# Output projection's first terms inside the context attention, and its norm, the quantised linear and the next norm as one stage worked by halves

## The reference

```python
x = x + xattn0(layernorm(x), ctx)      # causal attention, then attention to the context, 16 heads of 16; output projection Wp, bp
x = x + linear0(layernorm(x))          # FP6 (E2M3) block-quantised linear: 256 -> 256
x = x + attn1(layernorm(x))            # hyperbolic attention; starts with W_qkv

def _mx_quantize(t, eps=1e-30):        # blocks of 32 elements share a scale
    scales = jnp.maximum(jnp.max(jnp.abs(blocks), axis=-1) / FP6_E2M3_MAX, eps)
    q = _nearest_on_grid(blocks / scales[..., None], _GRID)
out = xd @ wd.T + bias                 # xd, wd: quantised and scaled back
```

## Time and profile before

| | us |
|---|---|
| median of three runs (4047.57 to 4056.62) | 4048.33 |
| the profiled execution's own time | 4053.46 |
| its span, first to last instruction | 4051.7 |
| from the divide's last instruction (L1335) to De's first product (L2122), batch 1 | 46.74 |
| TensorE matmul busy over the span | 3359.0 (83%) |
| VectorE busy over the span | 2079.9 (51%) |
| ScalarE busy over the span | 1633.4 (40%) |
| GpSimd busy over the span | 919.6 (23%) |

### The profile page before, as it was taken

The page is one execution under the profiler, slowest core; times in us unless marked ns, Lnnn a source line. Parts: engine busy times, 40 slices in busy tenths (PEclk is TensorE's granted clock), DMA queues, the critical chain, the costliest instruction groups (busy, mean ns, idle before and its releaser), DMA issues. The chain is left out here.

```text
span 4051.7 us, 56156 instructions
## 1 busy us (share of the span) xinstructions
PE 3359.0 (83%) x21550; PEld 1837.2 (45%) x21550; DVE 2079.9 (51%) x4231; ACT 1633.4 (40%) x2349; POOL 919.6 (23%) x961
## 2 busy tenths in 40 slices
PE   6887788988887788988887888988876888947997
PEld 4325545254334535254234543263254452436886
DVE  5655665634655665634746555535656556430111
ACT  3353833333445642433437542433538333411221
POOL 1202822011105522012116420012018220140111
PEclk9998799999997898999997998999997999958998
DMA  4102012011202022011220121012120121134554
GB/s 116 55 13 78 1 45 89 20 38 45 59 24 55 1 49 84 20 43 40 59 69 11 32 71 51 19 24 60 38 78 1 45 72 37 35 126 159 172 180 150
DMA packets 227190, 239.73 MB, mean 59 GB/s; under 512 B 95542, under 2 KB 193956, under 8 KB 224612
## 3 DMA queue, kind: packets, MB, share of 16 engines
q1 hardware_dynamic: 219552, 215.73, 18.3%
q10 hardware_dynamic: 3620, 10.07, 0.7%
q0 software_dynamic: 3744, 10.26, 0.7%
HBM read 167.24 MB, written 68.76 MB: 58 GB/s over the span
## 5 line engine op out<-in xcount | busy, mean ns | idle before, releaser
L867 ACT ACTIVATE prob<-psum 128x1024 f32<-128x1024 f32 x384 | 372.2, 1021 | 509.0 <-PE psum L785 509.0
L1235 ACT ACTIVATE prob<-psum 128x1024 f32<-128x1024 f32 (+3 forms) x384 | 331.6, 914 | 363.8 <-PE psum L1136 363.8
L913 DVE TENSOR_REDUCE scr<-psum 128x1 f32<-128x512 f32 x576 | 369.0, 685 | 195.9 <-PE psum L772 192.1
L1275 DVE TENSOR_REDUCE stats<-psum 128x1 f32<-128x512 f32 (+3 forms) x576 | 331.9, 619 | 140.9 <-PE psum L1124 137.7
L782 PE MATMUL psum<-stack 32*128 32x512 f32 x1536 | 226.5, 660 | 15.2 <-ACT prob L867 10.4
L398 PE MATMUL psum<-ident 128*128 128x128 f32 x1704 | 213.5, 280 | 0.0
L398 PEld LDWEIGHTS psum<-ident 128*128 128x128 f32 x1704 | 203.7, 195 | 14.9 <-issue 13.8
L1124 PE MATMUL psum<-stack 96*128 96x512 bf16 (+3 forms) x576 | 181.8, 364 | 31.5 <-DVE stats L1275 31.1
L815 PE MATMUL psum<-prob,ones_f 128*32 128x512 f32 x1536 | 202.1, 594 | 0.0
L1151 PE MATMUL psum<-prob,vbig 128*32 128x512 f32 (+3 forms) x1536 | 189.4, 566 | 4.2 <-ACT prob L1235 4.2
L2832 PE MATMUL psum<-xgT,ew 128*128 128x256 f32 x736 | 167.8, 387 | 18.0 <-DVE xgT L2880 18.0
(11 more groups left out here) (483 smaller groups left out, 6495.9 us busy)
## 6 DMA issues: line engine op xcount, KB each, us to landing
ew<-in_L_ffn_W SPq DMA_DIRECT2D x46, 1024.0 KB, 7.8
stack<-q_terms SPq DMA_DIRECT2D x144, 128.0 KB, 2.5
w_mlp<-in_L_xattn_a_li_w SPq DMA_DIRECT2D x16, 1024.0 KB, 6.2
q_terms<-parts SPq DMA_DIRECT2D x96, 128.0 KB, 2.2
stack<-k_terms SPq DMA_DIRECT2D x72, 128.0 KB, 2.9
stack<-k_terms SPq DMA_DIRECT2D x36, 256.0 KB, 4.4
w_mlp<-a_terms SPq DMA_DIRECT2D x36, 256.0 KB, 4.7
a_keys<-stack SPq DMA_DIRECT2D x4, 2048.0 KB, 6.3
```

What stands on the lines that cost most here:

```text
L867: act.activation(prob[:, i % 4, :, :], psum[:, 2 * p:2 * p + 2, :], ACT.Exp, scale=scale).then_inc(exped, 1)
L913: dve.tensor_reduce(found[:, c:c + 1], ring(i), AX.X, ALU.max).then_inc(freed, 1)
L1235: act.activation(prob[:, i % 4, :, q0:T], psum[:, 2 * p:2 * p + 2, q0:T], ACT.Exp, scale=scale).then_inc(exped, 1)
L1275: dve.tensor_reduce(found[:, c:c + 1], ring(i)[:, 0:keys_of(t)], AX.X, ALU.max).then_inc(freed, 1)
```

## The change

1. Of the 16 products of the output projection, the 12 for head groups 0 to 2 move into the last group of the context attention (`join_attention`): two ahead of each of the last four `weigh`, and four in place of `keep_running` beside the division. The bias row is added on GpSimd early in the same stage (`add_bias`).
2. `norm("Bo")`, "Cq" and `norm("Co")` become one stage "Cq". Two barriers go. The last four products of the output projection open it; the projections of keys and values follow at once.
3. The norms, the transposes, the copies and the products of the linear are done by halves of two tiles. VectorE joins two tiles with one instruction. The linear's bias is added on GpSimd beside the quantising.
4. `quantise` handles a list of parts, here two halves in turn, and `chained(..., behind=1)` waits for the instruction before the last, which belongs to the same half. Six instructions behind the rounding become four. The set-up's use of `quantise` on the weight gets the shorter form in one part.
5. Fillers on TensorE: 20, then 10, 4 and 6 of `keep_running`, in place of 11 and 5.

```diff
@@ -70,14 +70,15 @@
-def chained(eng, sem):
...
     def then(ins):
         count[0] += 1
         ins.then_inc(sem, 1)
-        eng.wait_ge(sem, count[0])
+        if count[0] > behind:
+            eng.wait_ge(sem, count[0] - behind)
     return then
@@ -224,36 +225,47 @@
...
-    def quantise(dve, then, src, n, a, b_, c_, amax, scale, rscale):
...
-        then(dve.tensor_scalar(src, a, MAGIC, None, ALU.add))
-        then(dve.tensor_scalar(src, src, MAGIC, None, ALU.subtract))
-
-        then(dve.tensor_tensor(b_, src, a, ALU.subtract))
-        then(dve.tensor_scalar(b_, b_, 0.5, None, ALU.is_ge))
-        then(dve.tensor_tensor(src, src, b_, ALU.subtract))
-        then(dve.tensor_tensor(src, src, c_, ALU.mult))
-        then(dve.tensor_tensor(s3, s3, scale.unsqueeze(2).to_broadcast(wide3), ALU.mult))
+    def quantise(dve, then, settled, parts, done):
...
+        for src, n, a, b_, c_, amax, scale, rscale in parts:
+            then(dve.tensor_reduce(amax, blocks(src), AX.X, ALU.max, apply_absolute_value=True))
...
+        for src, n, a, b_, c_, amax, scale, rscale in parts:
+            then(dve.tensor_scalar(src, a, MAGIC, None, ALU.add))
+        for src, n, a, b_, c_, amax, scale, rscale in parts:
+            then(dve.scalar_tensor_tensor(b_, src, MAGIC, a, ALU.subtract, ALU.subtract))
+        for src, n, a, b_, c_, amax, scale, rscale in parts:
+            then(dve.scalar_tensor_tensor(src, b_, 0.5, src, ALU.is_ge, ALU.subtract))
+        for src, n, a, b_, c_, amax, scale, rscale in parts:
+            then(dve.scalar_tensor_tensor(src, src, MAGIC, c_, ALU.add, ALU.mult))
+        settled()
+        for src, n, a, b_, c_, amax, scale, rscale in parts:
+            dve.tensor_tensor(blocks(src), blocks(src), per_block(scale, n), ALU.mult).then_inc(done, 1)
@@ -1182,14 +1195,25 @@
...
+                    if g == HG - 1 and kt >= 4:
+                        if kt == 4 and next_products:
+                            pe.wait_ge(divided, HG - 1)
+                        for t, k in next_products[2 * kt - 8:2 * kt - 6]:
+                            join_attention(pe, t, k)
                     weigh(n)
                     if kt == 2 and g:
                         spread_inverses(pe, g - 1, inverted, spread_in)
                     for ev in during[n][1]:
                         event(ev)
-                keep_running(pe, 3, 3)
+                for t, k in next_products[8:10]:
+                    join_attention(pe, t, k)
+                if not next_products:
+                    keep_running(pe, 3, 3)
                 gather(HG - 1)
-                keep_running(pe, 2, 3)
+                for t, k in next_products[10:]:
+                    join_attention(pe, t, k)
+                if not next_products:
+                    keep_running(pe, 2, 3)
                 spread_inverses(pe, HG - 1, inverted, spread_in)
                 keep_running(pe, 6, 3)
@@ -1245,6 +1269,8 @@
...
+                if beside is not None:
+                    beside(pool)
...
+    def join_attention(pe, t, k):
+        return pe.matmul(psum[:, 4 + t // 2, t % 2 * C:(t % 2 + 1) * C], yT[:, k, t * P:(t + 1) * P], wBp[:, k, :],
+                         start=(t % 2 == 0 and k == 0), stop=(k == HG - 1), skip_group_check=True)
@@ -2027,6 +2058,10 @@
...
+    def add_bias(pool):
+        for t in range(QT):
+            pool.tensor_tensor(x[:, t, :], x[:, t, :], e.R["L0_xattn_bp"], ALU.add)
...
+                   stack[:, 4096:12288].rearrange("p (s j n) -> p s j n", s=2, j=J), add=e.colB[:, 0, :], ready=ready,
+                   next_products=[(t, k) for t in range(QT) for k in range(HG - 1)], beside=add_bias)
...
+def fp6_linear(e):
...
+    with stage(nc, "Cq", "joined", "added", "var_ready", "rstd_ready", "dc", "normed", "biased", "quant", "turned", "xT_in", "summed",
+               "projected", "taken", "x_turned") as (
+            block, joined, added, var_ready, rstd_ready, dc, normed, biased, quant, turned, xT_in, summed,
+            projected, taken, x_turned):
         @block.sync
         def _(sp):
+            load_mlp(e, sp, 1)
             sp.wait_ge(taken, 2 * HG)
             sp.dma_start(e.a2_keys, e.work[:, 4096:8192]).then_inc(e.a2_stored, 16)
             sp.wait_ge(taken, len(jobs))
             sp.dma_start(e.a2_values, e.work[:, 0:4096]).then_inc(e.a2_stored, 16)
         @block.tensor
         def _(pe):
+            def turn(h, bank):
+                for k in range(KT):
+                    for t in HALVES[h]:
+                        c = k * N + t % 2 * P
+                        last = pe.transpose(psum[:, bank, c:c + P], xh[:, t, k * P:(k + 1) * P], ident[:, :])
+                return last
+            for h in range(2):
+                for t in HALVES[h]:
+                    last = e.join_attention(pe, t, HG - 1)
+                last.then_inc(joined, 1)
             pe.wait_ge(e.kv_loaded, 32)
             for i, (kind, g, h) in enumerate(jobs):
                 if i >= 4:
                     pe.wait_ge(taken, i - 3)
+                bank = psum[:, i % 4, :]
                 if kind == "k":
                     last = pe.matmul(bank, e.w2k[:, 0, g * P:(g + 1) * P], e.cnT[:, 0, h * BANK:(h + 1) * BANK],
                                      start=True, stop=True)
                 else:
                     last = pe.matmul(bank, e.cnT[:, 0, g * P:(g + 1) * P], e.w2v[:, 0, :], start=True, stop=True)
                 last.then_inc(projected, 1)
+            pe.wait_ge(taken, len(jobs))
+            e.keep_running(pe, 20, 0)
+            for h in range(2):
+                pe.wait_ge(quant, h + 1)
+                turn(h, 6 + h).then_inc(turned, 1)
+            for h in range(2):
+                pe.wait_ge(xT_in, h + 1)
+                pe.wait_ge(added, h + 1)
+                for t in HALVES[h]:
+                    for k in range(KT):
+                        last = pe.matmul(of_half(h)[:, t % 2, :], xT[:, k, t * P:(t + 1) * P], e.wC[:, k, :],
+                                         start=(t % 2 == 0 and k == 0), stop=(k == KT - 1), skip_group_check=True)
+                last.then_inc(summed, 1)
+            for h in range(2):
+                e.keep_running(pe, (10, 4)[h], 0)
+                pe.wait_ge(normed, 2 * QT - 2 + 2 * h)
+                turn(h, 6 + h).then_inc(x_turned, 1)
+            e.keep_running(pe, 6, 0)
         @block.scalar
         def _(act):
             for i, (kind, g, h) in enumerate(jobs):
                 act.wait_ge(projected, i + 1)
+                bank = psum[:, i % 4, :]
                 if kind == "v":
                     act.copy(values[:, g, :], bank).then_inc(taken, 1)
                     continue
                 act.copy(keys[:, g, h * BANK:(h + 1) * BANK], bank).then_inc(taken, 1)
+            for h in range(2):
+                act.wait_ge(turned, h + 1)
+                act.copy(xT[:, :, h * N:(h + 1) * N], psum[:, 6 + h, :].rearrange("p (k n) -> p k n", k=KT)).then_inc(xT_in, 1)
+            for h in range(2):
+                act.wait_ge(x_turned, h + 1)
+                act.copy(xT[:, :, h * N:(h + 1) * N], psum[:, 6 + h, :].rearrange("p (k n) -> p k n", k=KT))
+        @block.gpsimd
+        def _(pool):
+            def inverse_root(n, h):
+                pool.wait_ge(var_ready, n)
+                s = slice(2 * h, 2 * h + 2)
+                pool.tensor_tensor(rstd[:, s], eps_var[:, s], e.nhalf[:, 0:2], ALU.pow).then_inc(rstd_ready, 1)
+            inverse_root(1, 0)
+            inverse_root(2, 1)
+            for h in range(2):
+                pool.wait_ge(normed, 2 * h + 2)
+                for t in HALVES[h]:
+                    ins = pool.tensor_tensor(x[:, t, :], x[:, t, :], R["L0_ffn_bias"], ALU.add)
+                ins.then_inc(biased, 1)
+            inverse_root(3, 0)
+            inverse_root(4, 1)
+        @block.vector
+        def _(dve):
+            counted = [0]
+            then = chained(dve, dc, 0, counted)
+            then_other_half = chained(dve, dc, 1, counted)
+            def join(h):
+                dve.tensor_tensor(tiles(x, h), of_half(h), tiles(x, h), ALU.add).then_inc(added, 1)
+            def variance(h, n):
+                dve.wait_ge(added, n)
+                for t in HALVES[h]:
+                    last = dve.bn_stats(stats[:, t, :], x[:, t, :])
+                then(last)
+                for t in HALVES[h]:
+                    last = dve.bn_aggr(mv[:, t, :], stats[:, t, :])
+                then(last)
+                s = slice(2 * h, 2 * h + 2)
+                dve.tensor_scalar(eps_var[:, s], mv[:, s, 1], EPS, None, ALU.add).then_inc(var_ready, 1)
+            def normalise(h, n):
+                dve.wait_ge(rstd_ready, n)
+                for t in HALVES[h]:
+                    dve.tensor_scalar(xh[:, t, :], x[:, t, :], mv[:, t, 0:1], rstd[:, t:t + 1],
+                                      ALU.subtract, ALU.mult).then_inc(normed, 1)
+            for h in range(2):
```

(17 more changed lines are left out.)

95 lines of the change are left out of this document (48 added, 47 removed).

## The result

The changed kernel takes 3992.97 us, the median of four runs (3988.82 to 3995.69), beside 4052.47 us for the kernel before on the same chip (4047.57 to 4057.63). The ratio is 0.9853, with a 95% interval from 0.9839 to 0.9867. The profiled execution took 3994.16 us with a span of 3992.4.

What follows compares the result with a forecast made beforehand. Bound by a serial chain between barriers: last products and join, VectorE's norm and quantising, then a relay between engines. Four batches at 8.8 us plus 3 for the clock gave 38 off 4048.33: 4010 us, range 3998 to 4028.

Steps and rivals of the forecast that it cites:

- Rival B: TensorE's clock drops behind the quantising after 2.4 us idle: 5 us a batch, 4030 us if in all; chance 0.10.
- The clock in De: Next stage opens mostly at 2.4 GHz: 1.75 us saved in two batches, 3.5, of which 3 us booked.
- 4 x 8.8: Gain per batch in four batches: 3.8 us at the quantising's start, 2.0 in it, 3.0 behind it.
- A's spacing: Quantising halves do not overlap, instructions 0.73 and 0.46 us apart: 3.2 us more a batch, 4023 us; chance 0.11.
- C's steps of over 3.2 us: Early products in the context attention's last group do not hide: 2.6 us a batch, 4020 us; chance 0.03.
- E's queue: TensorE's in-order work in the stage, at 1.2 GHz throughout, ends 16.6 us a batch later: 4115 us; chance 0.04.
- D's loss: A later wait takes back the gain, so the change does nothing: 4036 to 4060 us; chance 0.06.
- GpSimd's work in a batch: Bias additions, 2.78 us on GpSimd, land where it was idle for 124.75 us: nothing booked.
- P: Follow-up theory: time outside the stage depends on where low-clock stretches fall against unchanged stages once a batch's length changes.

Runs made afterwards that it cites:

- a_pool14: Changed kernel with 14 tiny GpSimd instructions added in the context attention, where GpSimd is idle: 4004.4 us, ratio 0.9896.
- b_pool242: Kernel before with 242 tiny GpSimd instructions added in the context attention, where GpSimd is idle: 4039.13 us, ratio 0.9975.
- better: Changed kernel with early products one step earlier and by head group, linear's bias on GpSimd later, two fillers for four: 3977.74 us, ratio 0.9829.
- b_barrier: Kernel before with one semaphore cleared once more at the end of the second MLP unit: 4038.09 us, ratio 0.9974.
- wait_each: Changed kernel with each quantising instruction waiting for the one ahead, also across the halves: 4012.35 us, ratio 0.9917.
- after: The changed kernel itself, against the kernel before: 3992.97 us, ratio 0.9853.

## Why the prediction was off

**Right.** The stage opened 1.94 us after the divide. From there to the quantising 7.47 us passed (312.81 to 320.28), against 7.8. The instructions of the quantising are 0.61 and 0.34 us apart (322.08 to 323.30 for two, 324.50 to 325.17 for two), as taken from the one pair of neighbours that did not wait; half 0 was ready after 15.07 us (15.4 forecast), half 1 after 15.61 (16.0). The Trainium skill's VectorE: DVE Perf Modes, § Rules for kernel authors, would have instructions few rather than their waits. Here a wait one instruction back was worth 3.5 us a batch with the count unchanged, so on the waits the measurement speaks against it; on the count it agrees, for 32 short instructions with a wait on each took 19.1 us, where 18 long ones took 17.5. Behind the quantising the forecast had 12.2 us; batch 2 took 12.0, batch 1 13.5. Normalising beside the additions took 1.54 us, for a forecast 1.5. What the barriers that went are worth by themselves, no run shows; the sum over all the steps came out.

**Off in size, small.** The early products delay the last weighing by 0.99 us (300.94 to 305.13 is 4.19, against 3.20 in the earlier trace rows), not 0.6: between a score and a weighing two products take 1.06 us from start to start, not 0.86, and in the last step the pair started as the exponentials came. The context attention grew by 0.95 us a batch. Rival B came in part: the clock fell behind the quantising in two batches of four and cost 1.5 us each, where I had 5. The clock in De was sized at 3 us and the part up to Do gained 5.4; De's first four products take 1.95 or 1.96 us in all four batches. The stage and the context attention gained 36.9 - 3.8 = 33.1 us together, where 4 x 8.8 = 35.2 were forecast. That all this gives 38.5 for 38 is in part luck: one term was 2.1 too high and the other 2.4 too low. Of the other rivals, A's spacing, C's steps of over 3.2 us and E's queue did not show, and D's loss was a gain of the opposite sign.

**The step that failed** is the sum, "4 x 8.8 + 3 = 38 us": it books nothing for stages that the change doesn't touch, and the range goes down only by what could go better inside the stage. 20.8 us came from outside.

- 8 to 11 us: GpSimd's first instruction behind the loop's jump, late by 2.2 to 3.3 us a batch before and by 0.2 to 0.3 after, because its program is 14 instructions shorter. In the two profiled executions the three sections differ by 7.8 us together. `a_pool14`, which gives the lateness back, is 11.4 us slower than the changed kernel, and `b_pool242` 11.2 faster than the kernel before, of which its trace shows 5.9 in the sections. The prediction dealt with GpSimd's work in a batch ("nothing") and looked at no row of the next batch's first stage, where GpSimd's root starts 1.9 us after its variance is ready.
- The other 10 to 13 us stay open: 7.0 between the two MLP units, 1.9 in batch 1's first stage, 4.1 in the rest. Between the MLP units the same instructions took 223.2 to 223.7 us in 55 of the 80 batches of all 20 traces, and 224.9 to 227.0 in the other 25, `better`'s batch 2 (226.75) among them. The kernel before was long in three of its four batches, the changed kernel in none. But the kernel before and those made from it were long in 13 of 24 batches, with an average of 224.39 us, and the changed kernel and those made from it in 12 of 56, with 223.85. By these averages the change would win 2.2 us there, not 7.0; the rest is that these two executions fell far apart, as P has it. Why long batches are rarer with the change no run shows.

Open: which block of GpSimd's program is missing at the jump, and why 14 instructions decide it; the traces show one more load of instructions 0.2 to 0.9 us behind the branch at every jump of the six kernels that are late there (the five with 424 instructions, and `b_barrier`), and none ahead of 1.06 us in the other 14, not what it held.

## What to carry to other kernels

Work out the changed stretch from its rows, as here, and then ask two more things of a looped kernel: what each engine does right behind the loop's jump, and whether the edit changes the length of an engine's program. When a chain on VectorE is split into two independent halves, let each instruction wait for the one before the last: with a wait on each, the split chain was slower than the whole one (19.1 us against 17.5), and with the wait one back it was faster (15.6), with the first half ready another 0.5 us earlier for the next engine. Look for instructions to leave out first; two fewer were worth 1.45 us by the rows. Differences under some 10 us of 4000 between kernels whose batches differ in length say little, as long as TensorE's clock changes level inside them; read the stretch in the trace instead.

## What the runs showed of the hardware

- GpSimd was up to 3.4 us late behind a loop's jump, and the number of its instructions in the loop changed that: with 410 in a batch it was 0.2 to 0.3 us (13 traces), with 424 2.2 to 3.4 (5 traces), with 428 1.7, with 666 0.4 to 0.5. The Trainium skill, Advanced Engine Details and Errata, § ISA Cache, says that an engine other than TensorE keeps only two lines of 256 instructions. That would make the length of a loop matter as these runs show; what the engine held at the jump, no run shows. Its line of 16 KB agrees with the page of the changed kernel for one queue of instructions (177 packets, 2.90 MB) and not for the other (87 packets, 0.71 MB, 8.2 KB each), which is the one that loads behind GpSimd's branch; a packet need not be a line.
- TensorE's granted clock fell to 0.50, that is 1.2 GHz, under the linear's products of batch 1. It was 1.00 up to 336.60 us and 0.50 from 338 to 340; before that TensorE had run 4.7 us of fillers, idled for 1.43 us and run 1.26 us of transposes. In batch 2 the same idle time and the same rows came before, and it did not fall.
- Two chained VectorE instructions on 128x512 start 0.73 us apart when each waits for the one ahead (`wait_each`), and 0.60 to 0.61 when it waits for the one before that (`after`); two `tensor_scalar` 0.46 and 0.33 to 0.34.
